# A transformer tower on one core: the variance taken from 65 columns, mean steps on GpSimd, another order in the head

## The chip, the core and the metric

The kernel runs on one core of a Trainium2 chip. The time is the device time of one execution in microseconds; less is better. The core has five engines that run side by side and wait for each other by semaphores: TensorE (PE, matrix products into PSUM), VectorE (DVE), ScalarE (ACT), GpSimd (POOL) and SyncE (SP, which only issues transfers here).

## What is computed

Four lists of small integers (16 x 512 tokens) go through a token embedding, an attention layer and a layer of experts, all in float32 with 64 channels:

```
x   = [w*sin(ang), w*cos(ang)] of 4 periods x 3 harmonics        # 24 features a token
h2  = relu(x @ W1 + b1) @ W2 + b2
ln  = (h2 - mean(h2)) * rsqrt(var(h2) + 1e-5) * gamma + beta
h   = ln + 0.1 * (x @ Wres + bres)
n   = layernorm(h)                                                # (n - mean) / sqrt(var + 1e-5)
h   = h + attention(n)          # 8 heads of 64, one K and V for all, softmax over 512 keys, Wo
n   = layernorm(h)
h   = h + two of six experts (three 64x64 products each), weighed by a softmax router
```

Each token thus passes three norms: A in the embedding, B before the attention, and one before the experts (below: the unit's).

## The kernel before

The 16 sequences are worked in eight pairs of 1024 tokens. The loop `body(i, ...)` stands once for each engine and goes through the 64 slots of a pair. In slot c ScalarE forms the exponentials of score block c (`exps`, L915) with VectorE's negated row maximum (`maxima`, L1090). TensorE writes scores for two slots at a time (`scores`, L579), at every 16th slot the queries of the next heads (`queries`, L593), and for each head the weighted products in two parts (`pv`, L613). Between them lie, at slots given by the tables `P` (from pair 1 on), `P0` and `P1` (in the first pair) and `F`, the preparation of the pair after the next (`prep`: hidden layer, tokens, norms, transposed copy `T`, values) and the experts of the pair before (`ffn`). PSUM is a ring of four double banks; `ring_order` lists what takes a bank in order, and `read_at`, the slot from which each is read out, decides which bank is taken. Who takes a bank waits for the reader of the one before (`free`). The instructions of an engine run in the order in which they are written; a wait holds everything behind it on that engine.

The head stands ahead of the loops. The features are made in four column ranges (`four_cols`: 128, 384, 768 and 768 columns), each by three steps `reduced(..., n, step)` (L451, L455, L457), a sine (L1052) and `weigh` (L463). Tokens of the first sequence go through `first_tiles` on VectorE (L1164 to L1188): sum of squares, variance, power -0.5 on GpSimd (L1515), scale, residual, norm B. Then come the transposed copy (`first_copies`, L1205), the first queries and their copy `g` (L1207 on VectorE, L1074 on ScalarE), from which the first scores are made. Token blocks 0 and 1 (the two sequences of the first pair) and block 2 (the second pair) are done in the head by `tokens(w, step)`: hidden layer, residual, two halves of the second layer. `warm` is a row of products whose results nobody reads.

A norm in the loop has these steps: VectorE sums (`mean`, L1107) and multiplies by -1/64 (L1109); GpSimd centres (`centre`, L1446); ScalarE squares (L926, in A straight from the tokens, L934); VectorE sums the squares (`rstd`, L1115) and turns the sum into variance plus epsilon:

```
nc.vector.tensor_reduce(ln.st[:, 2, ln.tiles], ln.sq[:, ln.tiles, :], AX.X, ALU.add)          # L1115
nc.vector.tensor_scalar(ln.st[:, 3, ln.tiles], ln.st[:, 2, ln.tiles], 1.0 / C, LN_EPS, ALU.mult, ALU.add)   # L1117
```

GpSimd takes the power -0.5 (`deviation`, L1451) and scales (L1456); in norm A it also multiplies by gamma (L1466). GpSimd further makes `woz`, the output weights over the softmax sums (`over_sums`, L416), for which `pv` waits.

## Time and profile before

| | us |
|---|---|
| median of three runs (659.64 to 661.63) | 660.96 |
| the profiled run | 661.2 |
| its span in the trace | 659.3 |
| TensorE busy | 632.8 (96%) |
| VectorE busy | 529.0 (80%) |
| ScalarE busy | 476.6 (72%) |
| GpSimd busy | 278.7 (42%) |

The trace is of one execution, its times count from the span's start. "Idle before" is the time for which the engine stood still ahead of an instruction, and the name behind the arrow is what released it. PEld is TensorE's loading of weights, which lies beside its products. A matrix product of float32 appears as two records, so that a row "x8" is four products. A line with many instructions merges those that follow each other.

### The profile page before, as it was taken

The numbers are of one execution on the slowest core, as the hardware profiler recorded it, in microseconds if no ns is written. First come the engines' busy times: TensorE is split into PE (matmuls) and PEld (weight loads), VectorE is DVE, ScalarE is ACT, GpSimd is POOL, SyncE is SP. The second block draws the span as 40 slices with busy tenths as digits, with TensorE's granted clock in tenths as the row PEclk, the third lists the DMA queues.
The fourth block names the chain that finished last, engine by engine and source line by source line (L and its number), as shares of the span: only waits on it lengthen the run. The fifth ranks groups of instructions, "written<-read, shape, count | busy, mean of one in ns | idle before, by whom it ended". The sixth has DMA issues, their size and how long they took to land.

```text
span 659.3 us, 27475 instructions
## 1 busy us (share of the span) xinstructions
PE 632.8 (96%) x11948; PEld 363.8 (55%) x11948; DVE 529.0 (80%) x1069; ACT 476.6 (72%) x1215; POOL 278.7 (42%) x357
## 2 busy tenths in 40 slices
PE   7799999999999999999999999999999999999985
PEld 6355555546655565455665466555565556555663
DVE  6787877888697977979788887979869797878666
ACT  3888874986679775896658866787668966688543
POOL 2341313516463093623835155530836229131184
PEclk9999999999999999999999999999999999999999
DMA  5000000000000001000100001000010000000001
GB/s 179 2 2 2 2 3 3 3 2 3 18 2 3 2 2 19 2 2 3 19 2 2 2 3 20 2 2 2 3 19 1 3 3 6 15 2 2 3 4 34
DMA packets 9720, 6.79 MB, mean 10 GB/s; under 512 B 8704, under 2 KB 9088, under 8 KB 9472
## 3 DMA queue, kind: packets, MB, share of 16 engines
q1 hardware_dynamic: 9312, 4.77, 3.0%
q8 instruction: 94, 1.54, 1.0%
q10 hardware_dynamic: 288, 0.27, 0.1%
q14 instruction: 26, 0.21, 0.1%
HBM read 2.93 MB, written 2.10 MB: 8 GB/s over the span
## 4 chain that ended last, share of the span: by engine, by line
PE 84%; ACT 6%; DVE 6%; issue 2%; DMA 1%; POOL 0%; SPq 0%; ACTq 0%; DVEq 0%; POOLq 0%
PE s_bank L613 33%; PE s_bank L579 29%; ACT p L915 4%; PE s_bank L712 3%; PE s_bank L804 3%; PE s_bank L793 3%; PE s_bank L830 3%; DVE nmax L1090 3%; PE s_bank L593 3%; PE s_bank L724 1%; PE s_bank L690 1%; PE s_bank L624 1%; DMA e2t<-ids 1%; PE s_bank L642 1%; ACT g L921 1%
## 5 line engine op out<-in xcount | busy, mean ns | idle before, releaser
L915 ACT ACTIVATE p<-s_bank,nmax 128x512 f32<-128x512 f32 x512 | 347.5, 693 | 134.5 <-DVE nmax L1090 129.4
L1090 DVE TENSOR_REDUCE nmax<-s_bank 128x1 f32<-128x512 f32 x512 | 323.2, 681 | 42.0 <-PE s_bank L579 41.3
L579 PE MATMUL s_bank<-kf,g 64*64 64x512 f32 x2048 | 256.5, 591 | 1.6 <-ACT p L915 1.4
L613 PE MATMUL s_bank<-p,woz 64*64 64x256 f32 x4096 | 246.0, 377 | 2.9 <-ACT p L915 2.9
L613 PEld LDWEIGHTS s_bank<-p,woz 64*64 64x64 f32 x4096 | 158.2, 133 | 108.2 <-issue 31.1
L416 POOL TENSOR_TENSOR woz<-cst,rz 128x256 f32<-128x256 f32 x126 | 74.7, 614 | 243.0 <-DVE rz L1096 243.0
L579 PEld LDWEIGHTS s_bank<-kf,g 64*64 64x64 f32 x2048 | 75.6, 133 | 88.0 <-issue 38.3
L915 ACT ACTIVATION_READ_ACCUMULATOR p<-s_bank,nmax 128x1 f32 x512 | 107.0, 209 | 0.0
L1102 DVE STREAM_TRANSPOSE m<-s_bank 128x512 f32<-128x512 f32 x64 | 45.8, 716 | 36.4 <-PE s_bank L613 36.4
L1451 POOL TENSOR_TENSOR st<-st,power 128x8 f32<-128x8 f32 (+3 forms) x25 | 38.6, 1544 | 37.4 <-DVE st L1117 37.4
L425 POOL TENSOR_TENSOR y<-y,gt 128x768 f32<-128x768 f32 x28 | 41.3, 1474 | 2.8 <-DVE y L1361 2.8
L593 PE MATMUL s_bank<-kf,qk 64*64 64x512 f32 x256 | 33.8, 592 | 1.5 <-ACT tok L956 1.2
L830 PEld LDWEIGHTS s_bank<-cst,e2t 64*64 64x64 f32 x1536 | 28.8, 135 | 10.2 <-issue 5.8
L433 POOL TENSOR_TENSOR ys<-y 128x384 f32<-128x384 f32 x30 | 30.2, 1006 | 8.9 <-DVE y L1373 6.7
L921 ACT COPY g<-s_bank 128x1024 f32<-128x1024 f32 x31 | 31.5, 1018 | 2.6 <-PE s_bank L593 2.6
L1446 POOL TENSOR_TENSOR xc<-hatt,st 128x512 f32<-128x512 f32 x7 | 7.3, 1043 | 60.1 <-DVE st L1109 60.1
L830 PE MATMUL s_bank<-cst,e2t 64*64 64x64 f32 x1536 | 29.1, 218 | 2.4 <-issue 2.0
L1361 DVE TENSOR_TENSOR y<-s_bank,cst 128x768 f32<-128x768 f32 x28 | 26.3, 943 | 2.2 <-PE s_bank L830 1.9
L804 PE MATMUL s_bank<-e1t,cst 64*64 64x512 f32 (+2 forms) x216 | 26.6, 550 | 1.3 <-ACT e2t L1001 1.2
L1346 DVE TENSOR_SCALAR e2t<-s_bank,cst 128x512 f32<-128x512 f32 x36 | 25.3, 743 | 1.2 <-PE s_bank L804 1.2
L793 PE MATMUL s_bank<-xt,cst 64*64 64x512 f32 (+2 forms) x216 | 25.7, 545 | 0.0
L990 ACT ACTIVATE e1t<-s_bank,cst 128x1024 f32<-128x1024 f32 x21 | 23.7, 1129 | 2.1 <-PE s_bank L793 2.1
(133 smaller groups left out, 522.5 us busy)
## 6 DMA issues: line engine op xcount, KB each, us to landing
tower_out<-o SPq DMA_DIRECT2D x16, 128.0 KB, 2.8
cst<-consts SPq DMA_DIRECT2D x1, 1102.0 KB, 8.6
e2t<-ids SPq DMA_DIRECT2D x1, 768.0 KB, 6.0
cst<-consts SPq DMA_DIRECT2D x1, 352.0 KB, 6.4
cst<-consts ACTq DMA_DIRECT2D x1, 256.0 KB, 3.7
e2t<-ids SPq DMA_DIRECT2D x1, 192.0 KB, 3.6
cst<-consts SPq DMA_DIRECT2D x1, 128.0 KB, 3.4
e2t<-ids SPq DMA_DIRECT2D x1, 64.0 KB, 2.1
```

The lines of the kernel that those rows point to most:

```text
L416: ops.tensor_tensor(woz[:, kept, four, :].rearrange("q (m h) c -> q m h c", h=2), k("wo").rearrange("q (m c) -> q m c", m=4)[:, 2 * n:2 * ...
L425: ops.tensor_tensor(yt, yt, gt[:, 8, two, :].unsqueeze(3).to_broadcast([128, 2, NE, C]), ALU.mult).then_inc(y_pool, 1)
L579: last = pe.matmul(double[half(q), 512 * r:512 * r + 512], g[half(r), a // 2 % 2, a % 2, first:first + 64], kf[half(r), par, a // 4, :], s ...
L593: last = pe.matmul(double[half(q), 512 * r:512 * r + 512], qk[half(r), 2 * (quad % 2) + q, :], kf[half(r), par, quad // 2, :], start=True, ...
L613: last = pe.matmul(bank("PV", i, a)[half(q), 512 * hh:512 * hh + 256], woz[half(r), kept, 2 * mm + hh, :], keys[:, q, :, :], start=(part = ...
L793: last = pe.matmul(double[half(q), 512 * r + 64 * t0:512 * r + 64 * t1], k("e1")[half(r), first:first + 64], xt[half(r), u.cols], start=Tr ...
L804: last = pe.matmul(double[half(c), 512 * r + 64 * t0:512 * r + 64 * t1], k("e2")[half(r), first:first + 64], e1t[half(r), e, 512 * c + 64 ...
L830: last = pe.matmul(double[half(q), 512 * c + C * x:512 * c + C * x + C], e2t[half(c), x, first:first + 64], k("e3")[half(c), C * x:C * x + ...
L915: nc.scalar.activation(p[:, 8 * kept + c % 8, :], bank("S", i, c - r)[:, 512 * r:512 * r + 512], ACT.Exp, bias=nmax[:, c % 16:c % 16 + 1], ...
L1090: nc.vector.tensor_reduce(nmax[:, c % 16:c % 16 + 1], bank("S", i, c - r)[:, 512 * r:512 * r + 512], AX.X, ALU.max, negate=True).then_inc( ...
L1102: nc.vector.transpose(m[:, b2, n:n + 2, :, :].rearrange("q h n o -> q h (n o)"), bank("PV", i, a)[:, :].rearrange("q (h x) -> q h x", h=2) ...
L1451: nc.gpsimd.tensor_tensor(ln.st[:, 4, ln.tiles], ln.st[:, 3, ln.tiles], power[:, ln.tiles], ALU.pow).then_inc(ln.steps, 1)
```

## The change

1. The buffer of squares has 65 columns a tile instead of 64. GpSimd writes epsilon into the 65th once, at the start. ScalarE squares with a scale of 1/8, so that the sum over the 65 columns is the variance plus epsilon. The step L1117 (L1166 in the head) is left out.
2. The multiplication by -1/64 in the norms (L1109) is done by GpSimd in `centre`, except in the last pair's units, where VectorE keeps it.
3. In the head the token numbers of the last two column ranges come in two transfers; the squares of the first tiles stand ahead of the second sine; `weigh` of range 1 stands inside `first_tiles`; GpSimd's long step is the conversion of range 3 and waits for the scale on VectorE, and the reductions that VectorE had of range 3 are spread otherwise. The copy `g` is all VectorE's, in three parts, and the first scores wait for the first part alone.
4. Token block 2 is taken out of the head: its hidden layer stands in slots 2 and 3 of the first pair, its other products in slots 8 to 10, its copy in slot 11 instead of 7. `warm` ahead of the transposition has 4 products instead of 10.

```diff
-WARM0, WARM, WARM_T = 9, (1, 10), 12
+WARM0, WARM, WARM_T = 9, (1, 4), 12
...
-    "LNB2_POOL": 49, "T": 55, "T_ACT": (55, 55), "V": 63, "V_ACT": (63, 63), "TOK_ACT": 7}
+    "LNB2_POOL": 49, "T": 55, "T_ACT": (55, 55), "V": 63, "V_ACT": (63, 63), "TOK_ACT": 11, "H1": 2,
+    "H1_ACT": 3, "TOK": (8, 9, 10)}
...
-        sq = [sb(f"sq{n}", [128, 8, C]) for n in range(2)]
+        sq = [sb(f"sq{n}", [128, 8, C + 1]) for n in range(2)]
...
-            load_columns(2, slice(2 * QT, GCOL))
+            load_columns(2, four_cols[2])
+            load_columns(3, four_cols[3])
...
             def scores(i, par, c):
                 a, mm = c // 8, c % 8 // 2
-                if c % 16 == 0:
+                if i == 0 and c == 0:
+                    pe.wait_ge(g_part, 1)
+                elif c % 16 == 0 or i == 0 and c == 4:
                     pe.wait_ge(gsb, QUADS * i + a // 2 + 1)
...
-                nc.scalar.activation(ln.sq[:, ln.tiles, :], ln.xc[:, ln.tiles, :], ACT.Square).then_inc(ln.squared, 1)
+                nc.scalar.activation(ln.sq[:, ln.tiles, 0:C], ln.xc[:, ln.tiles, :], ACT.Square,
+                                     scale=C ** -0.5).then_inc(ln.squared, 1)
...
-                nc.vector.tensor_reduce(ln.st[:, 2, ln.tiles], ln.sq[:, ln.tiles, :], AX.X, ALU.add).then_inc(ln.sums, 1)
-                dve.wait_ge(ln.sums, ln.sums_at(ln.own + 1))
-                nc.vector.tensor_scalar(ln.st[:, 3, ln.tiles], ln.st[:, 2, ln.tiles], 1.0 / C, LN_EPS, ALU.mult,
-                                        ALU.add).then_inc(ln.sums, 1)
+                nc.vector.tensor_reduce(ln.st[:, 3, ln.tiles], ln.sq[:, ln.tiles, :], AX.X, ALU.add).then_inc(ln.sums, 1)
...
             def centre(ln, x):
-                pool.wait_ge(ln.sums, ln.sums_at(2))
+                pool.wait_ge(ln.sums, ln.sums_at(1))
+                nc.gpsimd.tensor_scalar(ln.st[:, 1, ln.tiles], ln.st[:, 0, ln.tiles], -1.0 / C, None,
+                                        ALU.mult).then_inc(ln.meant, 1)
+                pool.wait_ge(ln.meant, ln.n + 1)
...
-            for n, at_dve in enumerate((2, 8)):
+            for n in range(2):
+                last = nc.gpsimd.memset((sq[0], sq[2])[n][:, :, C:C + 1], LN_EPS)
+            last.then_inc(eps_set, 1)
             pool.wait_ge(power_set, 1)
+            for n, at_dve in enumerate((1, 7)):
                 pool.wait_ge(first_dve, at_dve)
                 nc.gpsimd.tensor_tensor(st[n][:, 4, 0:4], st[n][:, 3, 0:4], power[:, 0:4], ALU.pow).then_inc(first_pow, 1)
                 if n == 0:
-                    reduced(pool, nc.gpsimd, 2, 2)
+                    pool.wait_ge(first_dve, 3)
+                    reduced(pool, nc.gpsimd, 3, 0)
```

What this makes of the order of the instructions, at three places. The line numbers of the changed kernel are some two to nine higher or lower than those of before.

VectorE in the head, before, from the numbers of range 2 to the scale (L1171); `sq` and `st` are the squares and the small columns of the norm, `e1t` holds the rounded turns:

```order
L451 TENSOR_SCALAR feat<-e2t,rates 128x768
L463 TENSOR_SCALAR feat<-e1t,cst 128x384
L455 TENSOR_SCALAR e1t<-feat 128x768
L1164 TENSOR_REDUCE st<-sq 128x4
L1166 TENSOR_SCALAR st<-st 128x4
L1167 TENSOR_TENSOR tok<-s_bank,cst 128x4x64
L451 TENSOR_SCALAR feat<-e2t,rates 128x768
L1171 TENSOR_TENSOR xc<-tok,st 128x256
```

And in the changed kernel, up to the same scale (now L1167):

```order
L453 TENSOR_SCALAR feat<-e2t,rates 128x768
L1162 TENSOR_REDUCE st<-sq 128x4
L1163 TENSOR_TENSOR tok<-s_bank,cst 128x4x64
L465 TENSOR_SCALAR feat<-e1t,cst 128x384
L1167 TENSOR_TENSOR xc<-tok,st 128x256
```

The variance step L1166 and two feature steps (L455 and the second L451) are gone from ahead of the scale, and `weigh` (L463, now L465) stands behind the reduction. Behind the norm, VectorE before, from the normalized tile to the first maxima:

```order
L1188 TENSOR_TENSOR xn<-xc,st 128x256
L457 TENSOR_TENSOR feat<-feat,e1t 128x768
L1205 COPY kf<-s_bank 128x32x8
L1207 COPY g<-s_bank 128x512
L1090 TENSOR_REDUCE nmax<-s_bank 128x1 x7
```

And in the changed kernel:

```order
L1184 TENSOR_TENSOR xn<-xc,st 128x256
L459 TENSOR_TENSOR feat<-feat,e1t 128x768
L1201 COPY kf<-s_bank 128x32x8
L457 TENSOR_SCALAR e1t<-feat 128x768
L459 TENSOR_TENSOR feat<-feat,e1t 128x768
L1205 COPY g<-s_bank 128x256
L1206 COPY g<-s_bank 128x256
L1207 COPY g<-s_bank 128x512
L1090 TENSOR_REDUCE nmax<-s_bank 128x1 x7
```

Two feature steps and two more copies stand there now.

ScalarE before, from the key copy to the copy of the second queries (L921):

```order
L1071 COPY kf<-s_bank 128x32x8
L1052 ACTIVATE e1t<-feat 128x768
L1074 COPY g<-s_bank 128x512
L915 ACT_TABLE_LOAD
L915 ACTIVATE p,z<-s_bank,nmax 128x512
L934 ACTIVATE sq<-tok 128x256
L915 ACTIVATE p,z<-s_bank,nmax 128x512 x7
L956 COPY tok<-s_bank 128x1024
L915 ACTIVATE p,z<-s_bank,nmax 128x512 x3
L921 COPY g<-s_bank 128x1024
```

And in the changed kernel (L922 is that copy):

```order
L1072 COPY kf<-s_bank 128x32x8
L1055 ACTIVATE e1t<-feat 128x768 x2
L916 ACT_TABLE_LOAD
L916 ACTIVATE p,z<-s_bank,nmax 128x512
L936 ACTIVATE sq<-tok 128x4x64
L916 ACTIVATE p,z<-s_bank,nmax 128x512 x3
L951 ACTIVATE h1t<-s_bank 128x1024
L916 ACTIVATE p,z<-s_bank,nmax 128x512 x7
L922 COPY g<-s_bank 128x1024
```

The hidden copy (L951) stands behind the fourth exponential, the copy of `g` is gone from here, and the token copy is behind the query copy.

VectorE in the second pair before, around the sum of squares of norm A and the variance step:

```order
L1090 TENSOR_REDUCE nmax<-s_bank 128x1 x6
L1115 TENSOR_REDUCE st<-sq 128x8
L1117 TENSOR_SCALAR st<-st 128x8
L1090 TENSOR_REDUCE nmax<-s_bank 128x1 x2
L1102 STREAM_TRANSPOSE m<-s_bank 128x512
L1096 RECIPROCAL rz<-z 128x8
L1090 TENSOR_REDUCE nmax<-s_bank 128x1 x5
```

The second to fourth row are the reduction, the variance step and the maxima behind it; in the changed kernel the variance step is missing, here and at each other norm.

## Rows read from the trace of the kernel before

**Rows 1.** A window: stretch, length, busy PE, PEld, DVE, ACT, POOL; clock, DMA.

```profile
260.00:340.00 80.00, 78.73 (x1460) 44.72 (x1456) 66.06 (x130) 59.73 (x154) 36.49 (x47) 1.00 0.03 6
```

**Rows 2.** Waits of TensorE from 100 to 600 us: total, times, longest.

```profile
PE s_bank L712 <- ACT g L921: 3.0, 5, 0.7
PE s_bank L613 <- ACT p L915: 2.9, 6, 0.7
```

**Rows 3.** Timeline of the head: start, length, engine, line, operation, [idle before].

```profile
6.79 0.96 PE L675 MATMUL s_bank<-cst,h1t 64*64 64x64 f32 x32
...
8.06 0.37 ACT L1061 ACTIVATE sq<-s_bank 128x256 f32<-128x256 f32 x1
8.09 0.68 DVE L451 TENSOR_SCALAR feat<-e2t,rates 128x768 f32<-128x768 int32 x1 [0.49 <-DMA e2t<-ids]
...
9.54 0.41 DVE L1164 TENSOR_REDUCE st<-sq 128x4 f32<-128x256 f32 x1
...
10.31 1.03 POOL L1515 TENSOR_TENSOR st<-st,power 128x4 f32<-128x4 f32 x1 [9.10 <-DVE st L1166]
...
11.31 1.81 POOL L457 TENSOR_TENSOR feat<-feat,e1t 128x768 f32<-128x768 f32 x1
...
11.44 1.97 DVE L1171 TENSOR_TENSOR xc<-tok,st 128x256 f32<-128x256 f32 x1 [0.37 <-POOL st L1515]
...
16.32 1.22 POOL L463 TENSOR_SCALAR feat<-e1t,cst 128x768 f32<-128x768 f32 x1
16.43 0.42 DVE L1188 TENSOR_TENSOR xn<-xc,st 128x256 f32<-128x256 f32 x1 [0.51 <-POOL st L1515]
16.77 1.58 DVE L457 TENSOR_TENSOR feat<-feat,e1t 128x768 f32<-128x768 f32 x1
...
18.38 0.84 ACT L1052 ACTIVATE e1t<-feat 128x768 f32<-128x768 f32 x1 [0.34 <-DVE feat L457]
...
19.98 0.69 DVE L1207 COPY g<-s_bank 128x512 f32<-128x512 f32 x1 [1.29 <-PE s_bank L593]
...
20.58 1.28 ACT L915 ACT_TABLE_LOAD   x1
```

**Rows 4.** Timeline of the first pair's start, all engines.

```profile
22.12 4.34 DVE L1090 TENSOR_REDUCE nmax<-s_bank 128x1 f32<-128x512 f32 x7 [1.46 <-PE s_bank L579]
...
22.85 0.69 ACT L915 ACTIVATE p<-s_bank,nmax 128x512 f32<-128x512 f32 x1 [0.98 <-DVE nmax L1090]
...
28.47 1.05 ACT L956 COPY tok<-s_bank 128x1024 f32<-128x1024 f32 x1
...
29.58 1.09 PE L593 MATMUL s_bank<-kf,qk 64*64 64x512 f32 x8 [1.15 <-ACT tok L956]
...
31.34 1.91 PE L613 MATMUL s_bank<-p,woz 64*64 64x256 f32 x32
...
31.45 1.02 ACT L921 COPY g<-s_bank 128x1024 f32<-128x1024 f32 x1
```

**Rows 5.** Timeline in pair 2, around the long L1117.

```profile
181.70 1.04 POOL L1446 TENSOR_TENSOR xc<-hatt,st 128x512 f32<-128x512 f32 x1 [8.93 <-DVE st L1109]
...
184.31 0.63 ACT L926 ACTIVATE sq<-xc 128x512 f32<-128x512 f32 x1
...
188.80 1.09 POOL L1466 TENSOR_TENSOR xc<-xc,cst 128x512 f32<-128x512 f32 x1
188.86 1.05 DVE L1117 TENSOR_SCALAR st<-st 128x8 f32<-128x8 f32 x1
...
194.44 1.74 PE L613 MATMUL s_bank<-p,woz 64*64 64x256 f32 x28 [0.46 <-ACT p L915]
```

**Rows 6.** Whole run: L1117 (ns min/median/max), and GpSimd's power on eight columns.

```profile
L1117 DVE TENSOR_SCALAR st<-st x25: 170/172/1083, 26.8 to 635.4; 128x8 f32<-128x8 f32 x21, 128x4 f32<-128x4 f32 x2, 128x6 f32<-128x6 f32 x1, 128x2 f32<-128x2 f32 x1
...
L1451 POOL TENSOR_TENSOR st<-st,power 128x8 f32<-128x8 f32 x21 | 34.5, 1644 | 15.1 <-DVE st L1117 15.1
```

**Rows 7.** A window at the very end, columns as in rows 1.

```profile
656.00:659.00 3.00, 0.00 (x0) 0.00 (x0) 0.84 (x2) 0.00 (x0) 0.65 (x2) 0.62 0.22 44
```

More of the change, by code:

```diff
@@ L128, in prep @@
     def prep(w, slot, f=P):
-        for name, first in (("H1", P["H1"]), ("TOK", P["TOK"][0]), ("T", f["T"])):
-            if slot == first and not (name in ("H1", "TOK") and w <= 2):
+        for name, first in (("H1", f["H1"]), ("TOK", f["TOK"][0]), ("T", f["T"])) if w > 1 else (("T", f["T"]),):
+            if slot == first:
                 order.append((name, w))
@@ L149, in ffn @@
                 order.append(("Y", u, j))
-    order.extend([("H1", 0), ("TOK", 0), ("H1", 1), ("TOK", 1), ("QK",), ("H1", 2), ("T", 0), ("TOK", 2), ("Q", 0, 0)])
+    order.extend([("H1", 0), ("TOK", 0), ("H1", 1), ("TOK", 1), ("QK",), ("T", 0), ("Q", 0, 0)])
     for i in range(PAIRS):
@@ L235, in sums_at @@
     def sums_at(self, k):
-        return (self.own + 2) * self.n + k
+        return (self.own + 1) * self.n + k
     def step_at(self, k):
@@ L358, in bank @@
             return ring[place[what][0]]
-        load_ids = [sem(f"load_ids{n}") for n in range(3)]
+        load_ids = [sem(f"load_ids{n}") for n in range(4)]
         load_four, load_w1, load_qk, load_tok, load_rest = [
@@ L363, in tower @@
         stored = sem("stored")
-        (rated, power_set, spare_set, sine, feats, qk_ps, qk_sb, weighed, first_dve, first_sq, first_pow, first_xn) = [
-            sem(x) for x in ("rated", "power_set", "spare_set", "sine", "feats", "qk_ps", "qk_sb", "weighed",
+        (rated, power_set, eps_set, spare_set, sine, feats, qk_ps, qk_sb, weighed, first_dve, first_sq, first_pow, first_xn) = [
+            sem(x) for x in ("rated", "power_set", "eps_set", "spare_set", "sine", "feats", "qk_ps", "qk_sb", "weighed",
                              "first_dve", "first_sq", "first_pow", "first_xn")]
@@ L376, in tower @@
         W_SUM, W_LAST = 5, 4
-        ln_sems = [[sem(f"{x}{n}") for x in ("ln_dve", "ln_step", "ln_sq")] for n in range(2)]
+        ln_sems = [[sem(f"{x}{n}") for x in ("ln_dve", "ln_step", "ln_sq", "ln_mean")] for n in range(2)]
         def token_norm(n, w):
-            return Norm(xc[n], sq[n], st[n], *ln_sems[n], n=w - 1, own=(0, 2)[n], count=3, tiles=slice(4 if w == 1 else 0, 8))
+            return Norm(xc[n], sq[n], st[n], *ln_sems[n], n=w - 1, own=(0, 1)[n], count=3, tiles=slice(4 if w == 1 else 0, 8))
         def tok_of(w):
@@ L390, in tower @@
             n = u if pair < PAIRS - 1 else 0
-            sums, steps, squared, *own = unit_sems[max(0, u - PAIRS + 2)]
-            one_norm = Norm(xc[2], sq[2], st[2], sums, steps, squared, n=n, own=2, count=3, tiles=slice(parts[0], parts[-1]))
+            sums, steps, squared, meant, *own = unit_sems[max(0, u - PAIRS + 2)]
+            one_norm = Norm(xc[2], sq[2], st[2], sums, steps, squared, meant, n=n, own=1, count=3, tiles=slice(parts[0], parts[-1]))
             units.append(Unit(u, pair, parts, f, n, pool0, dve0, one_norm, *own))
@@ L696, in prep @@
                 for step in range(4):
-                    if w > 2 and slot == (P["H1"], *P["TOK"])[step]:
+                    if w > 1 and slot == (f["H1"], *f["TOK"])[step]:
                         tokens(w, step)
@@ L962, in prep @@
                     squares(token_norm(1, w))
-                if slot == P["H1_ACT"] and w > 2:
+                if w > 1 and slot == f["H1_ACT"]:
                     hidden(w)
@@ L1058, in _ @@
             hidden(0)
+            act.wait_ge(tok_ps, 1)
+            nc.scalar.activation(sq[0][:, 0:4, 0:C].rearrange("q (r x) c -> q r x c", r=2), first_tokens[:, :, :, 0:C],
+                                 ACT.Square, scale=C ** -0.5).then_inc(first_sq, 1)
             sines(1)
-            act.wait_ge(tok_ps, 1)
-            nc.scalar.activation(sq[0][:, 0:4, :].rearrange("q (r x) c -> q r x c", r=2), first_tokens[:, :, :, 0:C],
-                                 ACT.Square).then_inc(first_sq, 1)
             hidden(1)
@@ L1067, in _ @@
             tokens_out(1)
-            hidden(2)
-            sines(2)
             act.wait_ge(t_ps, 1)
             nc.scalar.copy(*keys(0, 0, 0)).then_inc(kf_sb, 1)
+            sines(2)
             sines(3)
-            act.wait_ge(gps, 1)
-            nc.scalar.copy(g[:, 0, 1, :], bank("Q", 0, 0)[:, 512:1024]).then_inc(g_first, 1)
             body(0, 0, False, True)
@@ L1123, in centred @@
             def centred(ln, x):
-                dve.wait_ge(ln.sums, ln.sums_at(2))
+                dve.wait_ge(ln.sums, ln.sums_at(1))
+                nc.vector.tensor_scalar(ln.st[:, 1, ln.tiles], ln.st[:, 0, ln.tiles], -1.0 / C, None,
+                                        ALU.mult).then_inc(ln.meant, 1)
+                dve.wait_ge(ln.meant, 1)
                 nc.vector.tensor_tensor(ln.xc[:, ln.tiles, :], x, wide(ln.st[:, 1, ln.tiles]), ALU.add).then_inc(ln.steps, 1)
@@ L1454, in scale @@
             def scale(ln, dst, src):
-                pool.wait_ge(ln.steps, ln.step_at(ln.own // 2 + 1))
+                pool.wait_ge(ln.steps, ln.step_at(ln.own + 1))
                 nc.gpsimd.tensor_tensor(dst, src, wide(ln.st[:, 4, ln.tiles]), ALU.mult).then_inc(ln.steps, 1)
```

59 lines of the change are left out of this document (28 added, 31 removed).

## The prediction

> **What bounds the kernel now.** I read the windows first, then TensorE's waits, and only then the head. In the middle TensorE is busy 78.73 of 80 us [rows 1]. So in the middle an edit on another engine counts only where TensorE waits for that engine. Between 100 and 600 us there are two such waits, each once a pair: 3.0 us in five for the query copy (L712 behind L921), 2.9 us in six for the exponentials (L613 behind L915) [rows 2]. The rest of the idle time is head and tail. The head is a chain through VectorE and GpSimd up to the first exponential at 22.85; a phase follows in which ScalarE sets the pace, until the first weighted product L613 at 31.34, from where TensorE runs without a break [rows 3, 4]. Hence the sum: how much earlier does that first L613 start, and which of the waits behind it go.
>
> **Head, up to the first exponential.** The chain is square, reduce, power, scale, normalize, transposed copy, queries, copy, scores.
> - The square ran behind a sine and started at 8.06; its input was ready at 6.79 + 0.96 = 7.75. It now goes first: 7.79, plus 0.37 = 8.16. The reduction stood behind a stall for the token numbers (VectorE idle 0.49 before L451) and L451 itself (0.68); with the numbers in two transfers the first half is in by about 7.6, L451 ends at 8.28 and the reduction starts at 8.3 instead of 9.54 [rows 3]. If the half lands as late as the whole did, it starts at 8.8. I take 8.3; the late case costs 0.5.
> - L1166 goes (0.17 as L1117 below, with its handover 0.2): reduction 8.3 to 8.71, power 8.86 to 9.89, scale at 9.99 instead of 11.44. The feature step moved in between, L463, waits for the second sine; that now ends about 8.7, while VectorE comes to it at 9.15, so it hides in the 1.03 us of the power.
> - The scale L1171 took 1.97 for 256 columns where L1188, as large, takes 0.42. GpSimd's L457 ran from 11.31 to 13.12 beside it [rows 3]. In the changed kernel GpSimd waits for that scale before it takes its long step. So 9.99 + 0.42 = 10.41 instead of 13.41: 3.0 us earlier. GpSimd's new step is a conversion of 768 columns, bounded by its L463 (1.22) and L457 (1.81); it ends at 12.3 at the latest, when the second power wants to start (12.2), cost 0 to 0.1.
> - The normalized tile then comes at 13.42 to 13.84. TensorE's second token block starts 0.5 us later than before, since its features do, and ends about 12.8; four warming products instead of ten fill to 13.7, so TensorE is just in time. L457 behind it (1.58 beside GpSimd's L463) now runs with GpSimd idle: 0.17 plus 1 ns a column, as L1188 has it, is 0.96, to 14.8. From its end to the first query copy there were 19.98 - 18.35 = 1.63 us [rows 3]: queries in at 16.4.
> - Here VectorE has two more steps to do, L455 (about 0.56) and L457 (0.96), from 15.2 to 16.75, so 0.35 of the gain is given back. Then the 0.69 copy is split: scores start after 256 columns, at 17.25, and three copies end at 18.25. The scores need about 0.95, first maximum 18.25, first exponential near 18.95. The other road agrees: last sine 16.8 to 17.63, table load 1.28 to 18.93 [rows 3]. **First exponential 18.95 instead of 22.85: 3.9 us earlier.**
>
> **First pair, up to the first L613.** Before, L613 followed 8.49 us behind the first exponential. Now ScalarE has the hidden copy (1024 columns, 1.05 long as L956, some 0.91 in a row of operations) before the fifth exponential. The eighth was done when the token copy L956 started at 28.47, 5.62 behind the first, which is 0.66 for each of eight after 0.37 for a square; now it is done at 6.55. L956, which hid the reciprocal and the ninth maximum, has moved behind; these two, 0.2 and 0.7 with their handovers, now stand open: ninth exponential at 7.55. Three exponentials at 0.66 make 9.55. And the bank of the first L613 is now that of the queries, so it waits for the copy L921, 1.02: 10.6 [rows 4]. That is 2.1 us more than before, and **3.9 - 2.1 = 1.8 us** are left. The moved token products, 2.7 us of TensorE's time, lie in the same gaps (it stood 1.15 us before L593 alone), and cost nothing of their own. From here both kernels have the same work on TensorE. If the scores wait for the hidden copy longer than I say, each 0.1 us is 0.1 of the sum.
>
> **Middle.** In pair 2 L1117, the step from sum of squares to variance, took 1.05 us, beside GpSimd's multiplication by gamma L1466 [rows 5]. Its 21 runs on eight columns take 8.9 us [rows 6]; so long is one in each of pairs 1 to 6 (111.5 to 498.6 us), six of about 1.05, which leaves 0.17 for each of the other 15. The maxima behind it come that much later, the exponentials behind these, and 5.6 us later TensorE stands 0.46 before L613. Each of the six waits, 2.9 us in all, follows such a long L1117. The change takes L1117 out, since the sum over 65 columns is the variance. The reduction before it gets eight columns more, 8 ns at 1 ns a column (L1164, 0.41 for 256 [rows 3], and L1090, 4.34 for seven of 512 [rows 4], have that slope). VectorE then comes 0.9 to 1.1 us earlier to the maxima, the transposition still has to wait for the L613 that runs there, so some 0.5 to 0.8 reaches the exponentials, against a wait of 0.46. **Gain 2.9 us.** The wait for L921 stays: no step of a norm stands in its chain.
>   The Trainium skill (SBUF — State Buffer, Who interferes with whom) says that a VectorE operation with two SBUF inputs, or a tensor_scalar in its two-port mode, and a GpSimd operation exclude each other for the whole instruction. This case's rows agree for L1171 and L1117. By that rule the last L457 of the head collides with GpSimd's L463, the first rival below.
>
> The mean step moves to GpSimd, in fifteen of its seventeen places: on VectorE it was 0.17; a GpSimd operation on eight columns is between that and the 1.64 of L1451, a power; I take 0.35 [rows 5, 6]. The centring L1446 ended at 182.74 and its reader, the square, ran at 184.31: 1.5 us of cover, so nothing up to the upper end, 0.1 beyond. The tail keeps its order; the last norm hides behind the warming products. Taken as 0.
>
> **Sum.** 661.2 (profiled run) - 1.8 - 2.9 = 656.5. That run lies 0.2 above the median of the three, 660.96, so I say 656.3.
>
> **Rivals.**
> - *The last reduction collides* (or the transfer is late). GpSimd's L463 becomes ready at 15.9, 0.1 us behind the start of VectorE's last L457. Before, GpSimd was first and L457 ended 0.8 behind it. If it is first again, L457 ends at 17.9 and not 16.75: 1.15 lost, 657.5. For it: a margin of 0.1. Against it: VectorE is ready first.
> - *The table load holds longer.* Before, 0.99 us lay between the load's end (21.86) and the exponential, which waited for a maximum, so the row can't tell whether ScalarE was ready. Now nothing covers that: up to 0.95 lost, 657.3.
>   The Trainium skill (ScalarE: Activation LUTs, What ACT_TABLE_LOAD costs) puts 1.38 us of draining to each load; by that 1.4 would be lost. No row here shows it.
> - *The waits in the middle stay*: the transposition, and not the maxima, holds the chain, and only the head pays: 659.2.
> - *It does nothing*: the opened ScalarE chain of the first pair eats the whole head and the middle stays: 660.8.
> - *Slower by the clock.* Six warming products fewer and gaps between 16.4 and 24 let TensorE fall to 1.2 GHz. It did so in this trace only after some 3 us of rest, at the very end (0.62 in 656:659), and held 1.00 everywhere before [rows 7]; my longest gap is 1.1 us. If it ran at half for 20 us from there, it would lose 10 us of work, less 2.4 of slack in the first pair, less 4.7: 3 us slower, 664. It decides from about 14 us at the low level.
> - *More*: the L921 waits go too, 653.3.
>
> **Numbers.** Forecast 0.50 (its own range 655.3 to 657.3); the collision or the table 0.20; middle stays 0.14; nothing 0.05; clock 0.07; more 0.04. Range 654.8 to 660.0 leaves out the last three. A measurement tells 0.3%, 2 us, from no change: faster 0.74, the same 0.19 (third and fourth), slower 0.07.
>
> **What would show it.** Head: scale near 0.42 and ending about 10.4, first exponential at 18.9 to 19.0, first L613 at 29.6, hence 10.6 behind the exponential. Middle: no VectorE step of 1 us before the maxima, L613's waits for L915 gone, L921's as before. Wrong if a new TensorE wait appears once a pair, if the first L613 is later than 30.5, or if the granted clock falls in the head.

## The result, and the profile of the changed kernel

| | before | changed |
|---|---|---|
| median of twenty runs each, us | 660.29 (659.07 to 664.09) | 654.02 (653.39 to 659.5) |
| the profiled run | 661.2 | 659.5 |
| its span in the trace, and mean granted clock | 659.3, 0.998 | 657.7, 0.987 |

The ratio over all executions is 0.9928, with an interval of 0.9913 to 0.9943; times 660.96 that is 656.2, against a forecast of 656.3. It hides something, though: the medians of the table stand at 0.9905. The changed kernel's twenty executions fall into two groups: twelve at 653.4 to 654.6 with a mean granted clock of 0.996 to 0.999, and eight at 656.3 to 659.5 with 0.987 to 0.992. The profiled one is of the second group, so its trace can't simply be set beside that of before. Two windows of it (columns as in rows 1), and the head in windows of 5 us:

```profile
260.00:340.00 80.00, 79.44 (x1476) 45.45 (x1471) 66.34 (x126) 58.36 (x150) 37.40 (x49) 1.00 0.03 6
...
5.00:10.00 5.00, 3.05 (x70) 2.17 (x69) 4.25 (x14) 1.39 (x3) 0.65 (x1) 0.97 1.02 393
10.00:15.00 5.00, 4.91 (x72) 4.28 (x72) 3.87 (x15) 0.98 (x2) 2.48 (x3) 0.50 0.09 33
15.00:20.00 5.00, 4.36 (x60) 3.16 (x52) 1.76 (x4) 1.70 (x3) 0.35 (x1) 0.50 0.00 0
20.00:25.00 5.00, 4.46 (x40) 1.47 (x36) 3.05 (x7) 2.79 (x4) 2.15 (x2) 0.66 0.01 3
25.00:30.00 5.00, 3.69 (x56) 1.40 (x48) 3.91 (x7) 5.00 (x15) 1.42 (x2) 1.00 0.01 2
```

In the middle TensorE is busy 79.44 of 80 us, where it was 78.73 [rows 1]. In the head its clock stood at half, 1.2 GHz, from 9.7 to 23.4 us (0.97 in the first of these windows is 0.3 us at half, 0.66 in the fourth 3.4 us); before it was 1.00 there. The waits of TensorE from 100 to 600 us:

```profile
PE s_bank L717 <- ACT g L922: 2.9, 5, 0.7
PE s_bank L729 <- issue: 1.4, 1, 1.4
```

The wait for the query copy (now L922) is as in [rows 2], and the wait of the weighted products for the exponentials is gone from the list. The head, as it answers to [rows 3, 4]; L1167 is the scale that was L1171, L1184 the normalized tile, L916 the exponential and its table load, L618 the weighted products:

```profile
8.78 0.42 DVE L1162 TENSOR_REDUCE st<-sq 128x4 f32<-128x260 f32 x1 [0.57 <-ACT sq L1063]
9.12 0.41 DVE L1163 TENSOR_TENSOR tok<-s_bank,cst 128x256 f32<-128x256 f32 x1
9.36 1.02 POOL L1519 TENSOR_TENSOR st<-st,power 128x4 f32<-128x4 f32 x1 [8.06 <-DVE st L1162]
9.45 0.47 DVE L465 TENSOR_SCALAR feat<-e1t,cst 128x384 f32<-128x384 f32 x1
...
9.98 1.13 PE L647 MATMUL s_bank<-feat,cst 64*64 64x128 f32 x16 [1.75 <-DVE feat L465]
10.48 0.43 DVE L1167 TENSOR_TENSOR xc<-tok,st 128x256 f32<-128x256 f32 x1 [0.56 <-POOL st L1519]
...
13.93 0.43 DVE L1184 TENSOR_TENSOR xn<-xc,st 128x256 f32<-128x256 f32 x1 [0.51 <-POOL st L1519]
...
15.22 2.07 PE L872 MATMUL s_bank<-spare 128*128 128x128 f32 x8
...
17.23 1.13 PE L695 MATMUL s_bank<-cst,xn 64*64 64x64 f32 x32
...
24.34 0.69 ACT L916 ACTIVATE p<-s_bank,nmax 128x512 f32<-128x512 f32 x1 [1.85 <-DVE nmax L1090]
...
34.92 1.31 PE L618 MATMUL s_bank<-p,woz 64*64 64x256 f32 x20 [0.48 <-ACT g L922]
```

The scale takes 0.43 and ends at 10.91, where it ended at 13.41. But TensorE, at half its clock, is then late: the normalized tile is ready at 14.36, and the transposition L695 starts at 17.23, behind the second token block and four warming products that take 2.07 us. So the first exponential came at 24.34, later than before. Still the whole kernel was 1.7 us faster than before in this very run.

The middle is best read from the first weighted product to the first combination of values (L712 before, L717 after) in the last pair. Before it stands at 557.89, behind a first weighted product at 31.34 [rows 4]; after:

```profile
557.70 1.12 PE L717 MATMUL s_bank<-m,v 32*64 32x256 f32 x32
```

That is 526.55 us against 522.78, 3.8 us less, and the later first weighted product (34.92 against 31.34) takes 3.6 of them back. Most of the 1.7 us of this run is in the stretch behind that combination: 100.0 us against 101.4. That is no gain to count on. Over the fourteen profiled executions below this last stretch takes 99.4 to 102.0 us; it is 101.4 and 99.4 in two kernels that have the same instructions there (before and experiment 3). What makes it vary has not been looked into; a span, or a single time, says nothing finer than that.

### The profile page after: what moved, and what is told of

It reads as the page before. It is cut to its first block, busy times and chain, and to the rows that moved or that the text cites. A ratio compares the mean times of both kernels' runs of the same rounds, so it can differ in the third digit from the quotient of the medians.

```text
span 657.7 us, 27431 instructions
## 1 busy us (share of the span) xinstructions
PE 636.6 (97%) x11936; PEld 365.8 (56%) x11936; DVE 522.1 (79%) x1030; ACT 476.0 (72%) x1214; POOL 279.1 (42%) x374
## 4 chain that ended last, share of the span: by engine, by line
PE 91%; ACT 4%; DVE 3%; issue 1%; POOL 0%; ACTq 0%; DVEq 0%; POOLq 0%
PE s_bank L618 33%; PE s_bank L584 32%; PE s_bank L717 3%; PE s_bank L598 3%; PE s_bank L798 3%; PE s_bank L835 3%; PE s_bank L809 3%; ACT p L916 2%; PE s_bank L872 1%; PE s_bank L695 1%; PE s_bank L729 1%; PE s_bank L647 1%; PE s_bank L629 1%; ACT g L922 1%; DVE nmax L1090 1%
## 5 line engine op out<-in xcount | busy, mean ns | idle before, releaser
L916 ACT ACTIVATE p<-s_bank,nmax 128x512 f32<-128x512 f32 x512 | 347.6, 693 | 132.1 <-DVE nmax L1090 131.9
L618 PE MATMUL s_bank<-p,woz 64*64 64x256 f32 x4096 | 245.0, 376 | 0.5 <-ACT g L922 0.5
L618 PEld LDWEIGHTS s_bank<-p,woz 64*64 64x64 f32 x4096 | 157.4, 133 | 105.1 <-issue 31.8
L916 ACT ACTIVATION_READ_ACCUMULATOR p<-s_bank,nmax 128x1 f32 x512 | 107.1, 209 | 0.0
L1444 POOL TENSOR_SCALAR st<-st 128x8 f32<-128x8 f32 (+1 forms) x15 | 3.6, 237 | 71.2 <-DVE st L1107 71.2
L922 ACT COPY g<-s_bank 128x1024 f32<-128x1024 f32 x31 | 31.5, 1017 | 2.6 <-PE s_bank L598 2.6
L717 PE MATMUL s_bank<-m,v 32*64 32x256 f32 x768 | 22.8, 377 | 2.9 <-ACT g L922 2.9
```

Of the source, the lines that this page charges most:

```text
L618: last = pe.matmul(bank("PV", i, a)[half(q), 512 * hh:512 * hh + 256], woz[half(r), kept, 2 * mm + hh, :], keys[:, q, :, :], start=(part = ...
L717: last = pe.matmul(bank("FIN", u.u, s2)[half(b2), 512 * q:512 * q + 256], v[quarter(g4), par, b2, n, :], m[quarter(g4), b2, :, n, :], star ...
L916: nc.scalar.activation(p[:, 8 * kept + c % 8, :], bank("S", i, c - r)[:, 512 * r:512 * r + 512], ACT.Exp, bias=nmax[:, c % 16:c % 16 + 1], ...
```

## Experiments

**1. The changed kernel again**, with nothing edited.

> The changed kernel as it is, for its spread and a second profile. In its profiled execution TensorE's clock was at 0.50 from 10 to 20 us and the first L618 came at 34.92. Theory A (the clock falls in the head in some executions only): the executions stand in two groups, about 653.5 to 654.6 with a mean clock of 0.996 or more and 656 to 659.5 with 0.987 to 0.992; a profile of the first group shows the first L618 at about 29.3 and 1.00 throughout the head. Theory B (the slower executions have another cause): a profile at full clock still shows the first L618 beyond 33.

Twelve executions: five at 652.7 to 654.3 (clock 0.996 to 0.999), seven at 657.4 to 659.1 (0.988 to 0.992); ratio 0.9936 [0.9912, 0.996]. The two groups are there again. The profiled execution is once more of the slower one, with 0.50 from 10 to 20 us, behind a rest of 1.75 us of TensorE. No execution of the faster group of this kernel was ever profiled.

**2. Ten warming products ahead of the transposition instead of four.**

```diff
-WARM0, WARM, WARM_T = 9, (1, 4), 12
+WARM0, WARM, WARM_T = 9, (1, 10), 12
```

> The changed kernel with ten warming products ahead of the transposition, as before, instead of four. Theory A1 (the six products that were taken out let the clock fall): no execution above 656, all near 654. Theory A2 (the fall begins before them, at 5 to 6 us in the profile, so that they only cost time): the slow executions are as frequent as with four and longer by what six more products take at the low clock, some 3 us (four took 2.07 there); the fast ones stay at 653.5 to 654.6, or come up to 1 us later if the products now end behind the normalized tile.

Median 658.14; four executions at 654.7 to 655.3 with 0.998, eight at 656.1 to 661.5 with 0.986 to 0.994; ratio 0.9962 [0.9941, 0.9984]. The group at the low clock is no rarer, and the six more products cost about 1.4 us when the clock is high. Putting the removed warming products back does not keep the clock up.

**3. The kernel before with four of them.**

```diff
-WARM0, WARM, WARM_T = 9, (1, 10), 12
+WARM0, WARM, WARM_T = 9, (1, 4), 12
```

> The kernel before with four warming products instead of ten, nothing else. Theory A1 (their number decides on the clock): executions fall into two groups, a part of them 3 us or more above 660.3. Theory A2 (their number does not matter): 659 to 661.6, as before, the same spread.

659.73, ratio 0.9998 [0.9984, 1.0012]: their number does nothing to the time there. In its profile the second block came behind a rest of 2.22 us, since the token numbers had landed 0.9 us later than in the trace of before, and the clock fell for 3.3 us (11.9 to 15.3), ahead of the four products (15.48), at a place where VectorE and not TensorE paces the head, so that it cost little. The clock is not quite as before, though: eight of these twelve executions have a mean of 0.994 or less, against 4 of 29 of the kernel before beside them. That is not explained.

**4. The norms alone** (points 1 and 2 of the change, on the head and the token block's place of before).

```diff
-                nc.vector.tensor_reduce(ln.st[:, 2, ln.tiles], ln.sq[:, ln.tiles, :], AX.X, ALU.add).then_inc(ln.sums, 1)
-                dve.wait_ge(ln.sums, ln.sums_at(ln.own + 1))
-                nc.vector.tensor_scalar(ln.st[:, 3, ln.tiles], ln.st[:, 2, ln.tiles], 1.0 / C, LN_EPS, ALU.mult,
-                                        ALU.add).then_inc(ln.sums, 1)
+                nc.vector.tensor_reduce(ln.st[:, 3, ln.tiles], ln.sq[:, ln.tiles, :], AX.X, ALU.add).then_inc(ln.sums, 1)
```

> The kernel before with the norm edits alone: 65 columns, no step from sum of squares to variance in the loop, mean steps on GpSimd; head and token block 2 as before. My theory: the six waits of L613 for the exponentials go, 0.5 us each by the list of waits, or 0.7 each as the pairs' distance in the trace says (77.4 before, 76.6 in the changed kernel): 3 to 4.3 us faster, 656.0 to 657.3. Rival (the middle's gain comes from the new ring or from ScalarE's other order): no gain, 660.3.

655.98 (654.84 to 657.88), ratio 0.9938 [0.9922, 0.9954]: 4.1 us by the ratio, the larger part of the gain. Of its waits from 100 to 600 us only these two are over 0.2 us, the weighted products' is gone:

```profile
PE s_bank L714 <- ACT g L923: 2.9, 5, 0.7
PE s_bank L726 <- issue: 1.1, 1, 1.1
```

**5. The norms alone, with a small VectorE step put back** behind the sum of squares, on eight columns and read by nobody.

```diff
                 nc.vector.tensor_reduce(ln.st[:, 3, ln.tiles], ln.sq[:, ln.tiles, :], AX.X, ALU.add).then_inc(ln.sums, 1)
+                dve.wait_ge(ln.sums, ln.sums_at(ln.own + 1))
+                nc.vector.tensor_scalar(ln.st[:, 2, ln.tiles], ln.st[:, 3, ln.tiles], 1.0, 0.0, ALU.mult, ALU.add)
```

> norms_only with one small VectorE step again behind the sum of squares, where the variance step was (it writes a row that nobody reads). Theory (the small step that GpSimd's gamma product holds up is the cause of L613's waits): the step takes about 1.05 us in six pairs, the six waits are back, 659.5 to 660.5. Rival (the gain of norms_only comes from the mean steps' move or from GpSimd's earlier power): the time stays at 656 to 657, though the step is long or is short.

660.24, ratio 0.9994 [0.9979, 1.0009]: the gain is gone. The step (first line: ns min/median/max) has the long and the short durations of L1117, and the wait is back:

```profile
L1118 DVE TENSOR_SCALAR st<-st x25: 169/172/994, 29.1 to 636.1; 128x8 f32<-128x8 f32 x21, 128x4 f32<-128x4 f32 x2, 128x6 f32<-128x6 f32 x1, 128x2 f32<-128x2 f32 x1
```
```profile
PE s_bank L615 <- ACT p L917: 2.4, 6, 0.4
```

One of the long ones, in pair 2, starts 0.13 us behind a GpSimd operation:

```profile
190.55 1.09 POOL L1473 TENSOR_TENSOR xc<-xc,cst 128x512 f32<-128x512 f32 x1
190.68 0.99 DVE L1118 TENSOR_SCALAR st<-st 128x8 f32<-128x8 f32 x1
```

Nobody reads the step's result and it signals no semaphore, so it is its place in VectorE's queue ahead of the maxima, and not the chain of the norm, that costs the time. That it is the six long steps, and not the short ones too, is read from the waits, each of which follows a long one; no run takes out only the six.

**6. The variance step alone**: as 4, with the multiplication by -1/64 back on VectorE.

```diff
                 nc.vector.tensor_reduce(ln.st[:, 0, ln.tiles], x, AX.X, ALU.add).then_inc(ln.sums, 1)
+                dve.wait_ge(ln.sums, ln.sums_at(1))
+                nc.vector.tensor_scalar(ln.st[:, 1, ln.tiles], ln.st[:, 0, ln.tiles], -1.0 / C, None,
+                                        ALU.mult).then_inc(ln.meant, 1)
```

> norms_only with the mean steps back on VectorE: of the norm edits only the 65th column. Theory: the whole gain of norms_only is the variance step's, since the mean steps took 0.17 us and no wait of TensorE stands behind them: 655.5 to 656.5. Rival: the mean steps bear a part of it (they stand right ahead of three maxima): 657 or more.

656.13, ratio 0.9927 [0.9908, 0.9946], as 4 within the intervals. The move of the mean step is worth nothing that intervals of 1.2 us can tell.

**7. Seven filling products in the place of the rest**: the changed kernel with `warm(7, ...)` between token blocks 0 and 1.

```diff
             for step in range(1, 4):
                 tokens(0, step)
+            warm(7, bank("H1", 1))
             tokens(1, 0)
```

> The changed kernel with seven more warming products between the first sequence's tokens and the second's hidden layer, where TensorE rests 1.75 us in the profile of the changed kernel and its clock falls at the end of that rest. Theory: that rest, 0.3 us longer than the 1.46 of before because the features come 0.5 us later, is what the clock falls on; filled, no execution has the low clock in the head, and all lie at 652.5 to 654.5 with 0.996 or more. Rival (the six products taken out ahead of the transposition, or the gaps behind it, let it fall): still a third to a half of the executions at 656 to 659. Second rival (the fill comes into the way of the second block): all at 654 to 656.

654.35 (653.65 to 655.84), ratio 0.9901 [0.9882, 0.992]; all five executions at 0.995 to 0.999; one lies 1.3 us above what was expected. This is the head that the prediction had worked out, in the trace:

```profile
8.63 0.42 DVE L1163 TENSOR_REDUCE st<-sq 128x4 f32<-128x260 f32 x1
...
9.83 0.67 PE L647 MATMUL s_bank<-feat,cst 64*64 64x128 f32 x16
10.33 0.42 DVE L1168 TENSOR_TENSOR xc<-tok,st 128x256 f32<-128x256 f32 x1 [0.56 <-POOL st L1520]
...
13.78 0.42 DVE L1185 TENSOR_TENSOR xn<-xc,st 128x256 f32<-128x256 f32 x1 [0.51 <-POOL st L1520]
...
15.95 0.96 DVE L459 TENSOR_TENSOR feat<-feat,e1t 128x768 f32<-128x768 f32 x1
16.24 2.62 POOL L465 TENSOR_SCALAR feat<-e1t,cst 128x768 f32<-128x768 f32 x2 [2.57 <-ACT e1t L1056]
...
16.94 0.84 ACT L1056 ACTIVATE e1t<-feat 128x768 f32<-128x768 f32 x1 [0.80 <-DVE feat L459]
...
17.80 1.28 ACT L917 ACT_TABLE_LOAD   x1
18.49 1.89 DVE L1091 TENSOR_REDUCE nmax<-s_bank 128x1 f32<-128x512 f32 x3 [0.32 <-PE s_bank L584]
...
19.22 0.69 ACT L917 ACTIVATE p<-s_bank,nmax 128x512 f32<-128x512 f32 x1
```
```profile
29.79 1.53 PE L618 MATMUL s_bank<-p,woz 64*64 64x256 f32 x24 [0.48 <-ACT g L923]
```

**8. The same with token block 2 back in the head** (as 7, with point 4 of the change undone but for the four warming products).

```diff
-            warm(7, bank("H1", 1))
...
+            warm(7, bank("H1", 1))
...
             tokens(1, 3)
+            tokens(2, 0)
             free("T", 0)
             warm(WARM[1], bank("T", 0))
             turned(0)
+            tokens(2, 1)
...
             queries(0, 0, 0)
+            tokens(2, 2)
+            tokens(2, 3)
```

> fill7 with token block 2 back in the head (hidden layer ahead of the transposition, residual behind it, second layer behind the queries, token copy in slot 7), the other head edits kept. Theory by the count in the prediction: the first L618 follows the first exponential by 8.5 us again and not by 10.6, but the scores wait for the block's products behind the queries (some 0.9 us) and the keys' copy for its residual: first exponential near 19.9, first L618 near 28.4 against 29.2, so the move of the block costs up to 1 us: 652.5 to 653.5 where fill7 has 653.4. Rival (the move is a gain): 654.5 or more.

653.37 (652.9 to 654.19), ratio 0.9885 [0.9865, 0.9905], 1.0 us below 7. The first exponential comes at 19.95 and the first weighted product 8.49 behind it, at 28.44, just as far behind as before the change [rows 4]; with the block moved it was 10.57. The intervals of 7 and 8 overlap, and the two spans are equal (652.5 and 652.4), since the last stretch was 1.3 us longer here. But the first weighted product, 1.35 us earlier, and experiment 12 say that moving the block cost about 1 us.

**9. Feature step ahead of the gamma product**, to shorten the rest without any filling.

```diff
-                done(tt(in_two(weighted), first_tokens[:, :, :, 0:C], gamma, ALU.mult))
                 weigh(dve, nc.vector, 1)
+                done(tt(in_two(weighted), first_tokens[:, :, :, 0:C], gamma, ALU.mult))
```

> The changed kernel with one order changed on VectorE: the feature step of range 1 (L465) ahead of the multiplication by gamma (L1163, 0.41 us). The features of token block 1 then come 0.3 to 0.4 us earlier, and TensorE's rest ahead of its second block shrinks from 1.75 to 1.4 us, without any added product. Theory R (the length of that rest decides the clock): the executions at a mean clock of 0.987 to 0.992 are gone or at most one in six; median 653.8 to 654.8, clock 0.995 or more. Rival P (the seven filling products of fill7 held the clock by their own work; a rest 0.35 us shorter does nothing): a third to a half of the executions still at 657 to 659.5. The power on GpSimd (1.02 us) covers both VectorE steps, so the scale should start within 0.1 us of where it did.

655.46, ratio 0.9929 [0.9908, 0.9951]; three executions at 653.8 to 654.2 with 0.996 to 0.999, three at 656.7 to 657.9 with 0.986 to 0.992. The rest became 1.43 us, shorter than the 1.46 of before, and the clock fell all the same:

```profile
9.73 0.94 PE L647 MATMUL s_bank<-feat,cst 64*64 64x128 f32 x16 [1.43 <-DVE feat L465]
```
```profile
10.00:12.00 2.00, 2.00 (x35) 1.67 (x27) 1.28 (x7) 0.60 (x1) 1.36 (x2) 0.50 0.33 132
```

Theory R, that the length of this rest decides, falls.

**10. Experiment 8 without the filling products.**

> block_back without the seven filling products: the changed kernel with only token block 2 put back into the head, the rest before the second block as in the changed kernel, 1.75 us. Both theories on the clock (its rest, or the filling products) expect the two groups again here: fast executions at 652.5 to 653.5, a third to two thirds of them 3 to 5 us above at 0.987 to 0.992. Should all executions stay at 0.995 or more, the low clock belongs to something that the moved block does behind it, and both fall.

One execution at 652.17 with 0.997, three at 655.3 to 656.1 with 0.991 to 0.994; median 655.54, ratio 0.9918 [0.9897, 0.994]. The group at the lower clock is back as expected, so the moved block is not needed for it.

**11. The norms alone, with the feature step one place later.**

```diff
-            weigh(dve, nc.vector, 1)
             reduced(dve, nc.vector, 2, 1)
+            weigh(dve, nc.vector, 1)
```

> norms_only (head of the kernel before) with the feature step L465 of range 1 behind the rounding step L457 of range 2 on VectorE. TensorE's rest ahead of its second block grows from 1.66 to about 2.2 us; nothing else in the head moves by more than 0.1 us. Theory R: the granted clock falls to 0.50 in the head in at least a third of the executions, mean clock below 0.993 there, and these are 1 to 4 us above the others (less than in the changed kernel, since VectorE and not TensorE paces this head); the others at 655.5 to 656.5. Rival P: no such group, all executions at 655 to 657 with 0.995 or more, as norms_only has them.

655.38 (654.57 to 655.7), ratio 0.9924 [0.9909, 0.994]. The rest did not grow as meant: the token numbers had landed early in the profiled execution (L453 started at 7.52, not at 8.32 as in experiment 4), and the rest was 1.48. Yet the clock fell from 11.2 to 14.6 us (0.81, 0.50 and 0.84 in the three windows of 2 us from 10 on), and two of four executions have 0.994. The head of before can fall too, and loses next to nothing by it. As a test of the rest's length the run is void.

**12. Experiments 8 and 9 together, with five filling products.**

```diff
-            warm(7, bank("H1", 1))
+            warm(5, bank("H1", 1))
...
-                done(tt(in_two(weighted), first_tokens[:, :, :, 0:C], gamma, ALU.mult))
                 weigh(dve, nc.vector, 1)
+                done(tt(in_two(weighted), first_tokens[:, :, :, 0:C], gamma, ALU.mult))
```

> block_back with the order of weigh_early on VectorE (L465 ahead of the gamma product) and five filling products instead of seven, so that the filled stretch ahead of the second token block is 1.3 us long instead of 1.83 and leaves no rest. weigh_early has refuted that a shorter rest alone holds the clock. Theory P (products in the place of the rest hold it, their number does not matter as long as the rest is gone): all executions at 0.995 or more, 652.5 to 654.3, median 653.2 (block_back: 653.37 with four executions, so this is also a second sample of that version). Rival C (the nine executions at the high clock with fill, in fill7 and block_back, were chance): with about half of the executions of the unfilled kernels at 0.994 or less, nine out of nine had a chance of 0.2%, and here some executions would lie 3 us higher, at 655.3 to 656.1 as in block_unfilled.

653.29 (652.31 to 654.22), ratio 0.9888 [0.987, 0.9907], all five at 0.995 to 0.999. Experiments 8 and 12 are the best versions; their intervals lie below that of the changed kernel (0.9913 to 0.9943), and they can't be told apart.

**All profiled executions together.** Times in us, each read from its trace; "rest" is TensorE's ahead of the second token block, "clock 8-28" the mean granted clock from 8 to 28 us, and "middle" is from the first weighted product to the first combination of values in the last pair.

```
                       rest   clock 8-28  first weighted  middle  span
before                 1.46   1.00        31.3            526.6   659.3
experiment 3           2.22   0.91        31.7            526.5   657.6
experiment 5           2.65   0.83        33.6            525.5   660.0
changed                1.75   0.66        34.9            522.8   657.7
experiment 1           1.75   0.66        34.7            522.4   657.1
experiment 2           1.75   0.74        35.3            521.8   658.0
experiment 4           1.66   1.00        31.6            521.6   654.1
experiment 6           2.18   0.83        33.2            521.6   656.0
experiment 9           1.43   0.83        32.3            522.5   654.9
experiment 10          1.75   0.83        32.1            522.7   654.3
experiment 11          1.48   0.91        30.8            521.7   653.5
experiment 7           none   1.00        29.8            522.0   652.5
experiment 8           none   1.00        28.4            522.0   652.4
experiment 12          none   1.00        28.6            522.1   651.5
```

The three kernels with a VectorE step behind the sum of squares have a middle of 525.5 to 526.6, the eleven without it 521.6 to 522.8. What the head does shows in the first weighted product. What a span has beyond these two is the last stretch, 99.4 to 101.4 with the step and 99.5 to 102.0 without it, so neither gives a gain there.

## Why the prediction was right, and where it was not

**Head up to the first exponential: right, where the clock holds.** Experiment 7 has the scale at 0.42, ending at 10.75 (forecast 10.41; the reduction started at 8.63, between the two cases 8.3 and 8.8), the tile at 13.78 (13.42) and the first exponential at 19.22 (18.95). The 0.3 us are those of the reduction.

**First pair: right.** 10.57 us from the first exponential to the first weighted product against 10.6, in the changed kernel's own trace 34.92 - 24.34 = 10.58. The parts are right too: in experiment 7 the ninth exponential starts at 26.72, 7.50 behind the first (forecast 7.55), and the query copy at 28.72, 9.50 behind (9.55). With the block in the head it is 8.49, so the 2.1 us that were counted against the move are real. The head's gain is 31.34 - 29.79 = 1.55, forecast 1.8.

**Middle: right in its cause, too small in its size.** Experiments 4 to 6 tie the gain to the one small step; the reduction with eight columns more takes 684 ns instead of 677, as forecast. The step of before that went, and the reduction after (busy, mean ns):

```profile
L1117 DVE TENSOR_SCALAR st<-st 128x8 f32<-128x8 f32 x21 | 8.9, 423 | 0.7
```
```profile
L1112 DVE TENSOR_REDUCE st<-sq 128x8 f32<-128x520 f32 x21 | 14.4, 684 | 3.7 <-ACT sq L936 3.7
```

The term that was mis-sized is "Gain 2.9 us", the sum of the six waits. The table gives some 522.0 against 526.5, so 4.5; against experiment 5 it is 3.5, and the ratios of experiments 4, 6 and 11 make 4.1, 4.8 and 5.0. In a steady stretch of four pairs the period was 77.44 before and is 76.76 (start of the same product in pairs 2 and 6):

```profile
175.48 0.89 PE L712 MATMUL s_bank<-m,v 32*64 32x256 f32 x22 [0.66 <-ACT g L921]
...
485.23 1.12 PE L712 MATMUL s_bank<-m,v 32*64 32x256 f32 x32 [0.66 <-ACT g L921]
```
```profile
178.69 1.12 PE L717 MATMUL s_bank<-m,v 32*64 32x256 f32 x32 [0.65 <-ACT g L922]
...
485.73 1.12 PE L717 MATMUL s_bank<-m,v 32*64 32x256 f32 x32 [0.56 <-ACT g L922]
```

That is 0.68 us a pair where the listed wait was 0.48. The prediction had worked out that 0.5 to 0.8 reach the exponentials, and then took the listed wait as the limit. It was none: from 180 to 500 us TensorE was busy 315.53 us before and is 317.75, so 2.2 us less idle or 0.54 a pair, and the rest lies in stretches that the trace counts as busy. What it is there has not been settled.

**Mean step: right.** GpSimd takes 237 ns for it (forecast 0.35), under 1.5 us of cover, and experiment 6 finds no effect:

```profile
L1444 POOL TENSOR_SCALAR st<-st 128x8 f32<-128x8 f32 x14 | 3.3, 237 | 69.8 <-DVE st L1107 69.8
```

**The collision and the table load did not come.** In experiment 7 VectorE's last L459 starts at 15.95, 0.29 ahead of GpSimd's L465, and takes 0.96; GpSimd is the one that waits: its first L465 takes 1.52, its second, with no such step of VectorE beside it, 0.98. In the changed kernel it is the same at 19.35 and 19.65. The margin had been put at 0.1. The table load stands from 17.80 to 19.08, right behind a sine that ends at 17.78, and the exponential starts 0.14 behind it. Even that is not the load's: the first maximum ends at 19.17, and the exponential follows it by 0.05, as it does elsewhere (0.04 in experiments 8 and 12). The 1.38 us of draining that the Trainium skill (ScalarE: Activation LUTs, What ACT_TABLE_LOAD costs) puts to each load are not to be seen here.

**The clock: the rival at 0.07 came true in about half of the executions, at another place and by another cause.** By the prediction's own signs of being wrong, two came in the changed kernel's trace: its first weighted product is later than 30.5, and the clock falls in the head. The step that failed is "my longest gap is 1.1 us". I had asked for gaps only behind the transposition, where warming products went, and had read the clock's fall off the one place where the trace of before had one, behind 3 us of rest. The gap that mattered was there in the trace of before, ahead of the second token block, and I had myself worked out that the features for which it waits come 0.5 us later. Its row, and the window behind it, of the kernel before:

```profile
9.21 0.67 PE L642 MATMUL s_bank<-feat,cst 64*64 64x128 f32 x16 [1.46 <-DVE feat L463]
```
```profile
10.00:15.00 5.00, 4.91 (x85) 4.03 (x78) 4.49 (x14) 3.27 (x5) 2.81 (x2) 1.00 0.04 12
```

There the clock held. A fall there costs the changed kernel 3 to 6 us, because its head waits for TensorE (L695 at 17.23 instead of 14.26). It costs the head of before less, because VectorE paces most of it: the first weighted product is at 31.7, 33.6 and 33.2 in experiments 3, 5 and 6, and part of this is the token numbers, which landed 0.8 to 1.2 us later there. The kernel before has such executions too: 12 of the 65 that ran beside the experiments have a mean clock of 0.990 to 0.994, at 661.1 to 663.1. By the prediction's own price, 664 for a fall of 20 us, the result would have been slower; the fall measured is 13.7 us long, just below the 14 us from which it said that rival decides.

**The cause of the fall is settled only in part.** Products in the place of the rest hold the clock: 14 of 14 executions (experiments 7, 8, 12) at 0.995 or more, against 25 of 54 without them (the changed kernel, experiments 1, 2, 9 and 10). They ran on other chips than experiments 1, 2, 9 and 10. The kernel before, run on all of these, was at 0.994 or less in 6 of 25 executions on the chips of the filled kernels and in 6 of 40 on the others, so the chip doesn't explain it. A mean of 0.995 rules out the long falls, but not surely one of 3 us. Ten warming products ahead of the transposition instead of four don't hold the clock (experiment 2); that their number has no part in it isn't shown (experiment 3). The length of the rest, between 1.43 and 1.75 us, doesn't decide: the clock held behind 1.46 and 1.66, and fell behind 1.43, 1.48 and 1.75. In all three traces with a rest of over 2 us (2.18, 2.22, 2.65) it fell, and there the rest was long because the token numbers landed late. Nor does the fall come at one place: it began within the rest in the changed kernel (at 9.7, the rest ended at 9.98), and 1.8 and 2.0 us behind its end in experiments 3 and 11. And it is not a property of the kernel alone, since the same kernel does both in turn. What tips one execution and not the next stays open.

**Sum.** Where the clock holds, -1.55 (head) and -4.5 (middle) from the 660.15 of the kernel before beside experiment 7 make 654.1; it measured 654.35, and the twelve faster executions of the changed kernel lie at 653.4 to 654.6; with the last stretch free by 2 us, so close a match is partly chance. The other eight gave 3 to 6 us back. That the ratio lands on 656.3 is thus partly luck: a middle sized too small by 1.6 us and a clock rival sized too small cancel.

## What to carry to other kernels

Price a small step by what is queued behind it on its engine, beside what another engine runs at that time: 170 ns became 1.05 us six times and cost some 4.5 us, and a sum over an added column takes it out. When a head is shortened until TensorE is what it waits for, look for every rest of TensorE in it, also those that cost nothing before, and time often enough to see two groups; a few products whose results nobody reads, put in the rest, kept the clock high in all 14 executions. A wait in the list of waits is not the limit of what its removal gives; compare the period.

## What the runs showed of the hardware

- The granted clock can fall to half around a rest of 1.43 to 1.75 us of TensorE and in the next execution of the same program not fall at all. In the changed kernel it stayed at half for 13.7 us, though TensorE was busy 4.91 and 4.36 us of five.
- A VectorE step on eight columns, whose result nobody reads, takes 169 ns alone and up to 994 ns beside a GpSimd operation on 512 columns. There GpSimd had started 0.13 us ahead. Where VectorE is first, by 0.29 us, it keeps its 0.96. The Trainium skill (SBUF — State Buffer, Who interferes with whom) has a VectorE operation with two SBUF inputs, or in a two-port mode, and a GpSimd operation exclude each other, and whoever issues first go through; these rows agree. The start in a trace doesn't always tell who was first: in the kernel before L1188 starts 0.11 behind GpSimd's L463 [rows 3] and keeps its 0.42, while L463 takes 1.22 instead of 0.98. In experiment 3 L457 starts 0.21 behind GpSimd's L463, right behind L1188, and takes 0.95; L463 takes 1.93.
- A table load of 1.28 us started 0.02 us behind the sine ahead of it, and an exponential 0.14 behind its end, 0.05 behind the maximum that it needs.
